# B and C products of a state space layer, taken by token quarters in four groups of 32 PSUM partitions

## The chip, the cores and the metric

The kernel is one program on one core of a Trainium2 chip. Its time is the device time in microseconds (us) of one execution; lower is better. Three runs of the kernel before gave a median of 1651.44 us, from 1648.73 to 1654.21.

## The reference, cut to what matters

A decoder layer works on x of shape (4, 1024, 256): a selective state space block, a cross attention over 154 context tokens and a mixture of eight experts, each behind a layer norm and each added to the stream. Only the first block's projections are touched:

```
xz = layernorm(x) @ W_in                 # 256 -> 1024, split into xp and z
xc = silu(causal_conv(xp))               # (4, 1024, 512)
Bm, Cm = split(xc @ W_x, 2)              # W_x is 512 x 32: 16 columns for B, 16 for C
dt = softplus(xc @ W_dt + b_dt)          # 512 x 512
h  = exp(dt * A) * h + (dt * xc) * Bm    # over 1024 tokens, 16 states for each of 512 channels
y  = sum over states of h * Cm, + D * xc
out = (y * silu(z)) @ W_out
```

## The kernel before, in words

The four batch rows are handled one after the other, in a software pipeline written out by hand. `over_rows` gives every engine the same frame: a phase for row 0, the loop of row 0, then for b = 1, 2, 3 a phase (which closes row b-1 and opens row b) and the loop of row b, then a phase that closes row 3, and the experts of row 3 alone. A phase does the matmul work outside the scan: for the closing row the gate and output products (Z, Y, O), the attention (T2, Q, PT, V), the expert input and the routing (N, G, CT); for the opening row the layer norm transposes (T), the input projection (X), the convolution, the products B, C and the step products S. The phase of row 0 has only the second part. The loop then goes over the 16 states: exponents on ScalarE, products with B on GpSimd, scans on VectorE, transposes on TensorE, sums with C on VectorE, ScalarE and GpSimd; the experts of the row before are woven in.

The order of matmul jobs in a phase is the list `all_jobs` (`alone_jobs` where no row opens); its end is `tail`. A job's PSUM bank is its place in the list modulo 8, except for those in `late_banks`. A counter `mm_ready` tells that a job is done. The reader of a job raises `act_freed` (ScalarE) or `dve_freed` (VectorE), and `wait_taken` waits for that: `wait_bank` does so for the last job in the same bank.

Around the change, in the order of `tail`:

- Job B, twice, one for each half of 512 tokens (`job_b`, L1598): `W_x` is the stationary operand, 128 rows by 32 columns for each of the four channel tiles (CT = 4), and 512 tokens of `xc` are moved past it; the sum over the four tiles stands in 32 partitions of a bank. One float32 `matmul` call becomes two weight loads and two matmul instructions in the trace, all under L1498 (`product`).
- ScalarE copies each half, 32 x 512, into `bc_sb` (L857), which is 32 partitions by 1024 tokens of `work`. Right behind these copies in ScalarE's order stand eight squares of the closing row (L863), then the exponents of the steps (L783), a table load and logarithms (L786, L789, L790), and the copies of the expert input (L800).
- Job C (`job_c`, L1609) waits for the second copy and makes eight transposes of 32 x 128 into 128 x 32 (L1615), so that tokens lie on partitions; VectorE copies the C half, 128 tokens by 8 tiles by 16 states, into `c_tok` (L1240).
- SyncE waits for the second copy, stores the 16 rows of B from `bc_sb` to `b_rows` in HBM with one DMA (L524), waits for its landing, and loads two rows of it, each broadcast to 128 partitions (`load_b`, L491), into `b_bc` and into the place of `w_out`. GpSimd waits for the first before its products `dtu` (L656).
- Eight jobs S (`job_s`, eight matmul instructions of 128 x 512 each, L1498) follow in TensorE's order. VectorE caps each (`cap`, L1113), ScalarE takes exp and ln, VectorE finishes the step (`step`, L1120). Between S jobs stand N, G and CT. In VectorE's order ahead of the first cap are the closing row's norm (L1085), the two `mean_square` (L1152), which wait for the squares, the `c_tok` copy between them, and eight instructions of the expert input (L1158), which wait for a reciprocal root on GpSimd (L619).

Of the kernel before, what the change touches and what calls it, by code (L numbers as in the profile page):

```python
# [16 lines left out]
ACT = mybir.ActivationFunctionType  # L17
# [3 lines left out]
P = 128  # L21
HALF = 512
# [6 lines left out]
def decoder_layer(nc, t, out):  # L29

    B, S, D = t["x"].shape
    DI = t["W_dt"].shape[0]
    N = t["A_log"].shape[1]
# [5 lines left out]
    DK, CT, TT = D // P, DI // P, S // P  # L39
    NH = S // HALF  # L40
# [5 lines left out]
    bd = nc.dram_tensor("b_rows", (B * N, S), F32, kind="Internal").ap()  # L46
# [9 lines left out]
    with ExitStack() as ctx:  # L56
        def sb(name, shape, dt=F32):
            return ctx.enter_context(nc.sbuf_tensor(name, shape, dt))
# [8 lines left out]
        w_x = sb("w_x", [P, CT, 2 * N])  # L67
# [14 lines left out]
        ident = sb("ident", [P, P])  # L82
# [9 lines left out]
        xc = sb("xc", [P, CT, S])  # L92
# [3 lines left out]
        c_tok = sb("c_tok", [P, TT, N])  # L96
# [4 lines left out]
        work = sb("work", [P, 10240])  # L101
# [26 lines left out]

        xp = dtu[:, :, :].rearrange("p a s -> p (a s)")[:, 0:2 * (PAD + S)].rearrange("p (r s) -> p r s", r=2)
        soft = work[:, 0:CT * NH * HALF].rearrange("p (r t) -> p r t", r=CT * NH)  # L130
        bc_sb = work[0:2 * N, 6912:6912 + S]
        TANH_AT = 8192
        NORM_AT = TANH_AT - 8 * TT
        stats = work[:, NORM_AT:NORM_AT + 6 * TT].rearrange("p (a n) -> p a n", n=6)
# [99 lines left out]
        b_stored = sem("b_stored")  # L234
# [11 lines left out]
        mm_ready = sem("mm_ready")  # L246
        act_freed = sem("act_freed")
# [50 lines left out]
        halves = range(NH)  # L298
# [4 lines left out]
        steps = [("S", d, c) for d in range(CT) for c in halves]  # L303
        LAST_STEP = CT * NH - 1

        def tiles_of(kind, c):

            if kind in ("O", "Q", "V"):
                return [(kind, c * TH + a, 0) for a in range(TH)]
            return [(kind, k, c) for k in range(CT if kind in ("Z", "Y") else DK)]  # L310

        def both(kind):
            return tiles_of(kind, 0) + tiles_of(kind, 1)

        head = [job for c in halves for kind in ("Z", "Y") for job in tiles_of(kind, c)] + both("O")
        tail = ([("B", 0, c) for c in halves] + [("C", 0, 0)] + steps[0:2] + tiles_of("N", 0) + steps[2:3] +
                tiles_of("N", 1) + steps[3:4] + [("G", 0, 0)] + steps[4:6] + [("CT", 0, c) for c in halves] + steps[6:])
        all_jobs = (head + both("T") + x_jobs((0, 1)) + both("T2") + x_jobs((2, 3)) + both("Q") + both("PT") +
                    both("V") + tail)
# [6 lines left out]
                      ("CT", 0, 0): 0, ("CT", 0, 1): 1}  # L326
        kinds_a = ("T", "X", "B", "C", "S")

        act_late = both("PT") + [("B", 0, c) for c in halves] + both("N") + [("CT", 0, c) for c in halves]
        act_order = both("T") + x_jobs((0, 1)) + both("T2") + x_jobs((2, 3)) + act_late  # L330
        act_alone = both("T2") + act_late
        dve_order = ([job for c in halves for kind in ("Z", "Y") for job in tiles_of(kind, c)] + both("O") +
# [54 lines left out]
        def wait_apart(eng, sem, value):  # L387


            eng.wait_ge(sem, value)  # L390
            eng.sem_inc(passed, 1)
# [64 lines left out]
        def _(sp):  # L456
# [38 lines left out]
            def phases(ph):  # L495
                r, b = ph.c_row, ph.a_row
                if r is not None:

                    wait_apart(sp, dbu_ready, (r + 1) * (N * CT) + DBU_CREDIT)
                    wait_apart(sp, hT_ready, (r + 1) * (N * TT) + HT_READY_CREDIT)  # L500
                    sp.dma_start(w_out[:, :, :].rearrange("p k n -> p (k n)"), w_outd).then_inc(w_out_loaded, 16)
                    load_x(r, xt, [xt_loaded, xt_loaded])
                    sp.dma_start(key_bias.rearrange("p (o f) -> p o f", o=1),
                                 k_rowd[bass.ds(r, 1), :].partition_broadcast(P)).then_inc(key_bias_loaded, 16)
                    sp.dma_start(kq[:, :, :], kqd[bass.ds(r * P, P), :].rearrange("p (k f) -> p k f", k=DK)
                                 ).then_inc(kv_loaded, 16)
                    sp.dma_start(vo[:, :, :], vod[bass.ds(r * KEYS, KEYS), :].rearrange("p (k f) -> p k f", k=2)
                                 ).then_inc(kv_loaded, 16)
                else:
                    sp.wait_ge(w_out_saved, 16)  # L510
                if r is not None and b is not None:

                    ph.wait_mm(sp, ("Y", CT - 1, NH - 1))
                    sp.sem_inc(passed, 1)
                    load_x(b, xn_a, x_in)
                if r is not None:

                    ph.wait_taken(sp, ("V", TT - 1, 0))
                    sp.dma_start(x2d[bass.ds(r * S, S), :].rearrange("(a p) d -> p a d", p=P),
                                 xt[:, :, :]).then_inc(x2_stored, 16)  # L520
                if b is not None:

                    ph.wait_taken(sp, ("B", 0, NH - 1))
                    sp.dma_start(bd[bass.ds(b * N, N), :], bc_sb[0:N, :]).then_inc(b_stored, 16)  # L524
                if r is not None:
                    wait_apart(sp, x2_stored, r * 16 + 16)
                if b is not None:
                    wait_apart(sp, b_stored, b * 16 + 16)
                    for par in range(2):
                        load_b(b, 0, 0, par)  # L530
                if r is not None:

                    ph.wait_taken(sp, ("CT", 0, NH - 1))
                    sp.dma_start(combd[bass.ds(r * E, E), :], rows[32:32 + E, :]).then_inc(comb_stored, 16)
                    wait_apart(sp, comb_stored, r * 16 + 16)
# [176 lines left out]
        def _(act):  # L712
# [52 lines left out]
            def phases(ph):  # L765
                r, b = ph.c_row, ph.a_row
# [53 lines left out]
                if r is not None:  # L820
                    for c in halves:
                        for job in tiles_of("Z", c):
                            d = job[1]
# [26 lines left out]
                if b is not None:  # L850
                    for d in (2, 3):
                        silu_tanh(d)
                    if r is None:
                        scale_weights()
                    for c in halves:
                        ph.wait_mm(act, ("B", 0, c))
                        act.activation(bc_sb[:, c * HALF:(c + 1) * HALF], ph.bank(("B", 0, c))[0:2 * N, :], ACT.Copy  # L857
                                       ).then_inc(act_freed, 1)
                if r is not None:
                    for a in range(TT):  # L860

# [36 lines left out]
                if b is None:  # L898

                    ph.wait_all_taken(act)  # L900
                else:

                    if r is not None:

                        wait_apart(act, x2_stored, b * 16)
                        wait_apart(act, x16_ready, b * TT)

                        wait_apart(act, b_stored, b * 16 + 16)

            def decay(b, alone, hf, it, par, d, opening=False, back=1):  # L910

# [134 lines left out]
        def _(dve):  # L1046
# [41 lines left out]
            def phases(ph):  # L1088
                r, b = ph.c_row, ph.a_row
# [71 lines left out]
                if r is not None:  # L1161
                    for c in halves:
# [6 lines left out]
                        for d in range(CT):  # L1169
                            job = ("Y", d, c)  # L1170
# [59 lines left out]
                if b is not None:  # L1230
                    if r is None:

                        dve.wait_ge(w_late, 7 * 16)
                        dve.tensor_scalar(w2[:, :], w2_raw, -0.5, None, ALU.mult).then_inc(dve_scaled, 1)
                        dve.tensor_copy(bias2[32:32 + E, :], bias2_raw[32:32 + E, :]).then_inc(dve_scaled, 1)
                        dve.tensor_scalar(bias1[:, :], bias1_raw[:, :], -1.0, LIMIT, ALU.mult, ALU.add
                                          ).then_inc(dve_scaled, 1)
                        dve.wait_ge(dve_scaled, 5)
                    ph.wait_mm(dve, ("C", 0, 0))
                    dve.tensor_copy(c_tok[:, :, :],  # L1240
                                    ph.bank(("C", 0, 0)).rearrange("p (a n) -> p a n", n=2 * N)[:, 0:TT, N:2 * N]
                                    ).then_inc(dve_freed, 1)
                if r is not None:
                    mean_square(1)
# [18 lines left out]
                if b is not None:  # L1263
# [13 lines left out]
                    _, d, c = steps[LAST_STEP]  # L1277
# [182 lines left out]
        def _(pe):  # L1460
# [35 lines left out]
            def product(bank, pairs):  # L1496
                for n, (left, right) in enumerate(pairs):
                    mm = pe.matmul(bank, left, right, start=(n == 0), stop=(n == len(pairs) - 1))  # L1498
                return mm
# [97 lines left out]
                mm.then_inc(mm_ready, 1)  # L1597

            def job_b(ph, r, b, job):
                c = job[2]  # L1600
                if r is None:
                    pe.wait_ge(w_early, 4 * 16)
                ph.wait_bank(pe, job)

                pe.wait_ge(xc_ready, b * CT + CT)
                product(ph.bank(job)[0:2 * N, :], [(w_x[:, d, :], xc[:, d, c * HALF:(c + 1) * HALF])
                                                   for d in range(CT)]).then_inc(mm_ready, 1)

            def job_c(ph, r, b, job):  # L1609

                ph.wait_bank(pe, job)
                ph.wait_taken(pe, ("B", 0, NH - 1))
                pe.sem_inc(passed, 1)
                for a in range(TT):
                    mm = pe.transpose(ph.bank(job)[:, a * 2 * N:(a + 1) * 2 * N], bc_sb[:, a * P:(a + 1) * P],  # L1615
                                      ident[0:2 * N, 0:2 * N])
                mm.then_inc(mm_ready, 1)

            def job_s(ph, r, b, job):
# [213 lines left out]
```

## Time and profile before

| | |
|---|---|
| median of three runs | 1651.44 us |
| the profiled execution's own time | 1651.05 us |
| span, first to last instruction | 1649.0 us |
| granted TensorE clock, mean | 0.892 |
| busy: TensorE, weight load | 1271.7 us, 839.9 us |
| busy: VectorE, ScalarE, GpSimd | 1404.2 us, 933.6 us, 969.9 us |

The span is the part of the execution between its first and its last instruction; 2.05 us lie around it. Busy times of engines overlap one another. In rows of a timeline, the first number is the start in us from the span's start, the second how long the merged group lasted, and what stands in brackets is how long the engine was idle before it and which engine, tile and line ended that. A matmul's duration includes its way through the array, so consecutive ones overlap in the records. "PE" is TensorE's matmul, "PEld" its weight load, "DVE" VectorE, "ACT" ScalarE, "POOL" GpSimd, "SP" SyncE.

### The profile page before, as it was taken

To read this page: it belongs to the slowest core of one execution; us is meant where nothing else is said; L and a number is where in the kernel's file an instruction comes from. 1 tells how busy PE (TensorE), PEld (TensorE's weight loads), DVE (VectorE), ACT (ScalarE), POOL (GpSimd) and SP (SyncE) were. 2 spreads that over 40 slices of the span, in tenths; PEclk is the share of its full clock that TensorE was granted. 3 is DMA by queue.
4 is the path that set the end of the run, shared out by engine and by line. 5 is a ranking of instruction groups with operands and counts; after the bars stand their busy time and mean duration, and the time that the engine had idled before them with its cause. 6 is when DMAs were issued, how large, how long until landed. Compare 5 with 4: busy or idle time off the path is not lost. (4 is left out here: it accounts for less than half of the span.)

```text
span 1649.0 us, 22776 instructions
## 1 busy us (share of the span) xinstructions
PE 1271.7 (77%) x5462; PEld 839.9 (51%) x5518; DVE 1404.2 (85%) x1861; ACT 933.6 (57%) x1373; POOL 969.9 (59%) x529
## 2 busy tenths in 40 slices
PE   4856667899677777899676777798877687796797
PEld 2334444564345554566354555566345454465465
DVE  6489999796899999787799999888789999973687
ACT  2454444144777777333777767523777767712554
POOL 1298888212889888321788979520588888620000
PEclk9977788999899899999899889999989989997699
DMA  7111110301111111101111111020111121010111
GB/s 226 40 39 39 39 39 26 105 1 53 59 58 38 58 52 57 62 27 54 39 59 52 44 59 63 8 87 28 65 39 58 42 67 51 25 61 26 44 59 51
DMA packets 54248, 86.47 MB, mean 52 GB/s; under 512 B 8380, under 2 KB 35141, under 8 KB 54158
## 3 DMA queue, kind: packets, MB, share of 16 engines
q1 hardware_dynamic: 50588, 83.20, 15.2%
q10 hardware_dynamic: 3570, 2.21, 0.4%
q8 instruction: 39, 0.64, 0.2%
q14 instruction: 51, 0.42, 0.1%
HBM read 74.83 MB, written 10.57 MB: 52 GB/s over the span
## 5 line engine op out<-in xcount | busy, mean ns | idle before, releaser
L1687 PE MATMUL ps<-ident,work 128*128 128x128 f32 x1536 | 307.6, 324 | 248.8 <-DVE stage L1330 169.2
L1292 DVE TENSOR_TENSOR_SCAN work<-ps,work 128x1024 f32<-128x1024 f32 x192 | 438.2, 2282 | 19.0 <-ACT ps L914 11.5
L1687 PEld LDWEIGHTS ps<-ident,work 128*128 128x128 f32 x1536 | 187.6, 159 | 385.1 <-DVE stage L1330 219.4
L914 ACT ACTIVATE ps<-dt,a_neg 128x1024 f32<-128x1024 f32 x256 | 284.7, 1116 | 116.6 <-DVE work L1292 95.1
L667 POOL TENSOR_TENSOR work<-dtu,b_bc 128x1024 f32<-128x1024 f32 x128 | 299.8, 2371 | 54.9 <-PE ps L1687 51.0
L1330 DVE SCALAR_TENSOR_TENSOR stage<-ps,c_tok,stage 128x512 f32<-128x512 f32 x384 | 271.9, 733 | 22.7 <-PE ps L1687 20.8
L1709 PE MATMUL ps<-w,work 128*128 (+1 forms) x1024 | 275.8, 419 | 2.0 <-DVE work L1437 2.0
L1709 PEld LDWEIGHTS ps<-w,work 128*128 128x128 f32 x1024 | 220.4, 217 | 54.1 <-issue 10.8
L1659 PE MATMUL ps<-nfT,w 128*128 128x512 bf16 x456 | 154.6, 429 | 40.7 <-DVE work L1367 14.8
L667 POOL TENSOR_TENSOR work<-dtu,w_out 128x1024 f32<-128x1024 f32 x64 | 149.2, 2353 | 42.1 <-PE ps L1687 42.1
L683 POOL TENSOR_TENSOR stage<-stage,work 128x512 f32<-128x512 f32 x128 | 160.1, 1275 | 14.5 <-ACT work L930 14.5
L619 POOL TENSOR_TENSOR rstd<-ve,minus_half 128x4 f32<-128x4 f32 x32 | 33.9, 1059 | 215.2 <-DVE ve L1078 198.7
L1292 DVE TENSOR_TENSOR_SCAN xt<-ps,xt 128x1024 f32<-128x1024 f32 x64 | 146.1, 2283 | 4.7 <-ACT ps L914 4.2
L667 POOL TENSOR_TENSOR xt<-dtu,w_out 128x1024 f32<-128x1024 f32 x64 | 149.8, 2362 | 0.0
L676 POOL TENSOR_TENSOR work<-work,wbc 128x1024 f32<-128x1024 f32 x48 | 112.8, 2349 | 37.0 <-DVE work L1367 37.0
L1498 PE MATMUL ps<-xnT,w_in 128*128 128x512 f32 x256 | 112.8, 594 | 2.1 <-DMA chan<-in_D_skip 1.8
L1498 PE MATMUL ps<-xc,w_dt 128*128 128x512 f32 x256 | 113.8, 597 | 0.7 <-ACT rows L887 0.7
L930 ACT ACTIVATE work<-ps,c_tok 128x512 f32<-128x512 f32 x128 | 81.9, 678 | 55.2 <-PE ps L1687 55.2
L1687 PE MATMUL ps<-ident,xt 128*128 128x128 f32 x512 | 110.0, 301 | 0.0
L1659 PEld LDWEIGHTS ps<-nfT,w 128*128 (+1 forms) x512 | 51.3, 105 | 95.3 <-issue 67.1
L656 POOL TENSOR_TENSOR dtu<-dt,xc 128x512 f32<-128x512 f32 x28 | 35.0, 1268 | 107.9 <-DVE dt L1120 107.9
L940 ACT ACTIVATE ps<-ps,bias 128x512 f32<-128x512 f32 x96 | 62.6, 652 | 40.3 <-PE ps L1659 40.3
(164 smaller groups left out, 1905.5 us busy)
## 6 DMA issues: line engine op xcount, KB each, us to landing
b_bc<-b_rows SPq DMA_DIRECT2D x32, 512.0 KB, 3.6
w_out<-b_rows SPq DMA_DIRECT2D x32, 512.0 KB, 3.9
wbc<-combine_rows SPq DMA_DIRECT2D x64, 256.0 KB, 3.3
stage<-in_x SPq DMA_DIRECT2D x8, 512.0 KB, 4.1
xt<-in_x SPq DMA_DIRECT2D x8, 512.0 KB, 6.1
x_rows<-xt SPq DMA_DIRECT2D x4, 1024.0 KB, 4.2
res<-x_rows SPq DMA_DIRECT2D x8, 512.0 KB, 3.9
out_x<-res SPq DMA_DIRECT2D x8, 512.0 KB, 3.6
```

The lines of the kernel that those rows point to most:

```text
L667: pool.tensor_tensor(slot(par, d), dtu[:, d, :], b_bcs[par], ALU.mult).then_inc(dbu_ready, 1)
L676: pool.tensor_tensor(ex_a, ex_a, wbc[:, 1 - par:2 - par, :].broadcast_to([P, 2, HALF]), ALU.mult).then_inc(aw_ready, 1)
L683: pool.tensor_tensor(stage[:, e, :], stage[:, e, :], evicted[:, e, :], ALU.add).then_inc(evict_added, 1)
L914: act.activation(decay_in(d, alone, opening), dt[:, d, :], ACT.Exp, scale=a_neg[:, bass.ds(it * 2 + (d * N + hf * (N // 2) + par), 1)]).th ...
L930: act.activation(evicted[:, e, :], ps[:, e % HT_BANKS, :], ACT.Copy, scale=c_tok[:, e, bass.ds(n, 1)]).then_inc(evict_ready, 1)
L940: act.activation(bank, bank, ACT.Relu, scale=-1.0, bias=bias1[:, bass.ds(it * 8 + (par * 4 + j), 1)]).then_inc(both_gate, 1)
L1292: dve.tensor_tensor_scan(h, decays, h, 0.0, ALU.mult, ALU.add).then_inc(scan_done, 1)
L1330: dve.scalar_tensor_tensor(stage[:, a, :], ps[:, a % HT_BANKS, :], c_tok[:, a, bass.ds(n, 1)], stage[:, a, :], ALU.mult, ALU.add).then_inc ...
L1498: mm = pe.matmul(bank, left, right, start=(n == 0), stop=(n == len(pairs) - 1))
L1659: mm = pe.matmul(ps[:, GATE_BANK + g, :], w1[:, bass.ds(wcol + k * 2 * I, P)], nfT[:, k, hf * HALF:(hf + 1) * HALF], start=(k == 0), stop= ...
L1687: mm = pe.transpose(ps[:, a % HT_BANKS, d * P:(d + 1) * P], slot(par, d)[:, a * P:(a + 1) * P], ident[:, :])
L1709: mm = pe.matmul(ps[:, 6 + a // 2, (a % 2) * D:(a % 2 + 1) * D], ex_a[:, j, a * P:(a + 1) * P], w2[:, bass.ds(col + j * D, D)], start=Fals ...
```

## The change

The four quarters of 256 tokens replace the two halves of 512. For each channel tile, four matmul calls with the same 32 weight columns move one quarter each, and quarter q goes to PSUM partitions 32q to 32q+31 of one bank. `bc_sb` becomes 128 partitions by 256 tokens and is filled by one copy. Two transposes of 128 x 128 take the place of eight of 32 x 128. The `c_tok` copy reads the same number of elements in another order. B is stored by four DMAs of 16 rows by 256 tokens, and who waited for one landing now waits for four. There is one job fewer in the list, so C moves from bank 6 to bank 5: the job S of bank 5 now waits for the `c_tok` copy, where N of bank 6 did.

```diff
-        bc_sb = work[0:2 * N, 6912:6912 + S]
+        QUARTERS = 4
+        QUARTER = S // QUARTERS
+        assert 2 * N * QUARTERS == P and QUARTER == 2 * P
+        bc_sb = work[:, 6912:6912 + QUARTER]
...
-        tail = ([("B", 0, c) for c in halves] + [("C", 0, 0)] + steps[0:2] + tiles_of("N", 0) + steps[2:3] +
+        tail = ([("B", 0, 0), ("C", 0, 0)] + steps[0:2] + tiles_of("N", 0) + steps[2:3] +
...
                 if b is not None:
-                    ph.wait_taken(sp, ("B", 0, NH - 1))
-                    sp.dma_start(bd[bass.ds(b * N, N), :], bc_sb[0:N, :]).then_inc(b_stored, 16)
+                    ph.wait_taken(sp, ("B", 0, 0))
+                    for q in range(QUARTERS):
+                        sp.dma_start(bd[bass.ds(b * N, N), q * QUARTER:(q + 1) * QUARTER],
+                                     bc_sb[q * 2 * N:q * 2 * N + N, :]).then_inc(b_stored, 16)
...
-                    wait_apart(sp, b_stored, b * 16 + 16)
+                    wait_apart(sp, b_stored, (b + 1) * (QUARTERS * 16))
...
-                    for c in halves:
-                        ph.wait_mm(act, ("B", 0, c))
-                        act.activation(bc_sb[:, c * HALF:(c + 1) * HALF], ph.bank(("B", 0, c))[0:2 * N, :], ACT.Copy
-                                       ).then_inc(act_freed, 1)
+                    ph.wait_mm(act, ("B", 0, 0))
+                    act.activation(bc_sb, ph.bank(("B", 0, 0))[:, 0:QUARTER], ACT.Copy).then_inc(act_freed, 1)
...
                     ph.wait_mm(dve, ("C", 0, 0))
-                    dve.tensor_copy(c_tok[:, :, :],
-                                    ph.bank(("C", 0, 0)).rearrange("p (a n) -> p a n", n=2 * N)[:, 0:TT, N:2 * N]
+                    dve.tensor_copy(c_tok[:, :, :].rearrange("p (q u) n -> p q u n", u=2),
+                                    ph.bank(("C", 0, 0))[:, 0:2 * P].rearrange("p (u q n) -> p q u n", u=2, q=QUARTERS
+                                                                               )[:, :, :, N:2 * N]
                                     ).then_inc(dve_freed, 1)
...
             def job_b(ph, r, b, job):
-                c = job[2]
...
-                product(ph.bank(job)[0:2 * N, :], [(w_x[:, d, :], xc[:, d, c * HALF:(c + 1) * HALF])
-                                                   for d in range(CT)]).then_inc(mm_ready, 1)
+                for d in range(CT):
+                    for q in range(QUARTERS):
+                        mm = pe.matmul(ph.bank(job)[q * 2 * N:(q + 1) * 2 * N, 0:QUARTER], w_x[:, d, :],
+                                       xc[:, d, q * QUARTER:(q + 1) * QUARTER], start=(d == 0), stop=(d == CT - 1))
+                mm.then_inc(mm_ready, 1)
...
-                ph.wait_taken(pe, ("B", 0, NH - 1))
+                ph.wait_taken(pe, ("B", 0, 0))
                 pe.sem_inc(passed, 1)
-                for a in range(TT):
-                    mm = pe.transpose(ph.bank(job)[:, a * 2 * N:(a + 1) * 2 * N], bc_sb[:, a * P:(a + 1) * P],
-                                      ident[0:2 * N, 0:2 * N])
+                for u in range(2):
+                    mm = pe.transpose(ph.bank(job)[:, u * P:(u + 1) * P], bc_sb[:, u * P:(u + 1) * P], ident[:, :])
                 mm.then_inc(mm_ready, 1)
```

## Rows read from the trace of the kernel before

**Rows 1.** Windows: us, busy (instructions) of PE, PEld, DVE, ACT, POOL; clock; DMA share; GB/s.
```profile
305.00:424.00 119.00, 109.84 (x436) 68.03 (x436) 91.25 (x228) 53.61 (x101) 32.67 (x24) 0.97 0.15 51
424.00:687.00 263.00, 193.62 (x893) 132.37 (x908) 247.02 (x230) 186.32 (x253) 219.03 (x110) 0.89 0.14 47
```

**Rows 2.** Timeline of TensorE in the phase before row 1's loop.
```profile
378.46 7.05 PE L1498 MATMUL ps<-xc,w_x 128*32 128x512 f32 x16
386.28 0.65 PE L1615 MATMUL ps<-ident,work 32*128 32x32 f32 x8 [0.77 <-ACT work L857]
386.86 7.13 PE L1498 MATMUL ps<-xc,w_dt 128*128 128x512 f32 x16
...
402.89 0.56 PE L1498 MATMUL ps<-gate_w,nfT 128*128 128x8 bf16 x16 [1.02 <-ACT nfT L800]
```

**Rows 3.** Timeline of ScalarE in the same stretch.
```profile
385.55 0.59 ACT L857 ACTIVATE work<-ps 32x512 f32<-32x512 f32 x1 [2.85 <-PE ps L1498]
386.04 0.40 ACT L863 ACTIVATE work<-xc 128x256 bf16<-128x256 bf16 x1
...
394.82 0.63 ACT L783 ACTIVATE work<-work 128x512 f32<-128x512 f32 x1 [0.81 <-DVE work L1113]
```

**Rows 4.** Timeline of VectorE in the same stretch.
```profile
383.69 1.38 DVE L1085 TENSOR_SCALAR xc<-xt,work,rstd 128x256 bf16<-128x256 f32 x4 [1.12 <-POOL rstd L619]
387.76 0.17 DVE L1152 TENSOR_SCALAR ve<-ssq 128x4 f32<-128x4 f32 x1 [2.70 <-ACT work L863]
...
389.36 0.17 DVE L1152 TENSOR_SCALAR ve<-ssq 128x4 f32<-128x4 f32 x1 [1.20 <-ACT work L863]
389.43 3.25 DVE L1158 SCALAR_TENSOR_TENSOR work<-xc,rstd,norm_w 128x256 bf16<-128x256 bf16 x8
392.60 0.74 DVE L1113 TENSOR_SCALAR work<-ps,chan 128x512 f32<-128x512 f32 x1
394.03 0.75 DVE L1113 TENSOR_SCALAR work<-ps,chan 128x512 f32<-128x512 f32 x1 [0.69 <-PE ps L1498]
...
401.91 0.75 DVE L1113 TENSOR_SCALAR work<-ps,chan 128x512 f32<-128x512 f32 x1 [2.42 <-PE ps L1498]
```

**Rows 5.** Groups of the whole trace, shapes apart: count, busy us, mean ns, idle before.
```profile
L1498 PE MATMUL ps<-w_out,xc 128*128 128x256 f32 x256 | 55.9, 379 | 0.0
L1498 PEld LDWEIGHTS ps<-w_out,xc 128*128 128x128 f32 x256 | 48.3, 190 | 6.4
L1506 PE MATMUL ps<-ident,stage 128*128 128x128 f32 x256 | 32.2, 280 | 15.4 <-DVE stage L1085 15.4
...
L1498 PEld LDWEIGHTS ps<-xc,w_x 128*32 128x32 f32 x64 | 7.0, 115 | 35.3 <-issue 35.3
...
L745 ACT ACTIVATE xc<-ps 128x256 f32<-128x256 f32 x2 | 0.8, 384 | 1.9 <-PE ps L1493 1.9
```

**Rows 6.** Timeline of GpSimd in the same stretch.
```profile
388.01 1.01 POOL L619 TENSOR_TENSOR rstd<-ve,minus_half 128x4 f32<-128x4 f32 x1 [4.36 <-DVE ve L1152]
...
398.25 2.50 POOL L656 TENSOR_TENSOR dtu<-dt,xc 128x512 f32<-128x512 f32 x2 [7.47 <-DVE dt L1120]
```

**Rows 7.** Timeline of SyncE's DMA issues in the same stretch.
```profile
386.31 0.36 SPq L524 DMA_DIRECT2D b_rows<-work  x1
388.74 0.37 SPq L491 DMA_DIRECT2D b_bc<-b_rows  x1
```

**Rows 8.** DMA issues of the page: count, KB each, median us to landing.
```profile
b_bc<-b_rows SPq DMA_DIRECT2D x32, 512.0 KB, 3.6
```

**Rows 9.** Timeline of row 0's phase: the B products, the first cap.
```profile
44.75 8.77 PE L1498 MATMUL ps<-xc,w_x 128*32 128x512 f32 x16 [14.22 <-DVE xc L1107]
...
58.56 0.75 DVE L1113 TENSOR_SCALAR work<-ps,chan 128x512 f32<-128x512 f32 x1 [3.27 <-PE ps L1498]
```

**Rows 10.** Windows of row 0's B products, columns as in group 1.
```profile
44.70:48.60 3.90, 3.85 (x5) 0.89 (x6) 2.57 (x3) 0.03 (x1) 0.00 (x0) 0.54 0.33 134
48.60:53.50 4.90, 4.90 (x12) 1.10 (x10) 0.00 (x0) 0.59 (x1) 0.00 (x0) 1.00 0.00 0
```

More of the change, by code:

```diff
@@ L327, in decoder_layer @@
         kinds_a = ("T", "X", "B", "C", "S")
-        act_late = both("PT") + [("B", 0, c) for c in halves] + both("N") + [("CT", 0, c) for c in halves]
+        act_late = both("PT") + [("B", 0, 0)] + both("N") + [("CT", 0, c) for c in halves]
         act_order = both("T") + x_jobs((0, 1)) + both("T2") + x_jobs((2, 3)) + act_late
@@ L906, in phases @@
                         wait_apart(act, x16_ready, b * TT)
-                        wait_apart(act, b_stored, b * 16 + 16)
+                        wait_apart(act, b_stored, (b + 1) * (QUARTERS * 16))
             def decay(b, alone, hf, it, par, d, opening=False, back=1):
```

## The prediction

> **What bounds the kernel now.** I read the table by stretches first, because whole-span busy shares mix two kinds of work. In a loop VectorE is busy 247 of 263 us and TensorE 194 at a lower clock; in the phase between two loops it is the other way round, TensorE 110 of 119 us at a clock of 0.97 and VectorE 91 [rows 1]. The edited jobs stand in the phases, so a microsecond saved there counts only if what follows in the phase moves with it, and the loop behind it, which cannot open before the phase's last step, then starts earlier by that much. So the second reading is the timelines of the engines from the B products to the router's products. TensorE runs almost without a gap: B from 378.46 to 385.51, 0.77 us idle for ScalarE's copy, the C transposes, then S products from 386.86 [rows 2]. Against it stand two other orders. ScalarE copies B's second half at 385.55, and eight squares sit behind that copy although their input was complete at 385.07 (383.69 + 1.38) [rows 3, 4]. VectorE waits for those squares twice (2.70 and 1.20 us), then forms the expert input, then caps S; the second cap waits 0.69 us for TensorE, the fourth 2.42 [rows 4]. So TensorE and the chain copy, squares, root, expert input, cap are nearly level here, and both begin at the end of B. In the phase of row 0 there is no closing row: the first cap waits 3.27 us for TensorE alone [rows 9].
>
> **The change, part by part.**
>
> *B products.* Removed are 16 matmul instructions of 512 columns (two halves, four channel tiles, two instructions per float32 call), added are 32 of 256 columns. Before, 7.05 us. A float32 instruction of 256 columns costs 55.9 / 256 = 0.218 us of TensorE's time, with a weight load of 0.190 us wholly beside it; its own record lasts 0.379 us, of which the rest is the way through the array [rows 5]. The trace has no case of two instructions in different column groups. So the bounds are: no overlap, 31 x 0.218 + 0.379 = 7.14 us; all four groups at once, 8 x 0.218 + 0.16 = 1.9 us; and above the first, every weight load exposed (0.115 us for 32 columns [rows 5]), 32 x (0.218 + 0.115) = 10.7 us. I take the middle kind: the groups can work side by side, but instructions start in order, and each call's second instruction must wait for its first, which uses the same group. Then the second of one quarter runs beside the first of the next, 16 turns instead of 32: 16 x 0.218 + 0.379 = 3.87 us, and B gets 3.18 us shorter. Why overlap at all: each instruction fills 32 of 128 columns, and time goes by the tokens moved, so three quarters of the array stand idle before. The nearest measured row (0.218, one after another) speaks for the other end, which is why that end keeps a good chance.
>
> The Trainium skill bears on this, for and against. Its page "TensorE: Matmul & The Clock Gate", section "Part 3: Packing small matmuls — row/col tiling", says that matmuls in different 32-column groups run concurrently while starting and ending in order, with 2.38 times the rate for three column groups; no row here shows it. By 2.38 alone B would take about 2.9 us as an estimate. Against: "TensorEngine Tiling (Array Packing)", section "Key Properties", says that a change of tiling mode drains TensorE; here the step from full-width products into the 32-column ones at 378.46 shows no idle time in the row, so I add nothing.
>
> *The copy.* Two of 32 x 512 (0.59 us each), of which the second is on the path, become one of 128 x 256: 0.384 us by a copy of the same size from PSUM [rows 3, 5]. 0.20 us saved.
>
> *C.* S starts 0.58 us after the first of eight transposes [rows 2]. Two of 128 x 128 take 2 x 32.2 / 256 = 0.25 us [rows 5]. 0.33 us saved. The `c_tok` copy has the same element count; I cost its new order at nothing, since VectorE waits for roots then anyway.
>
> *S on TensorE, middle phases.* 3.18 + 0.20 + 0.33 = 3.71 us earlier: S starts at 383.15, its second job ends at 390.28 (7.13 us [rows 2]).
>
> *The other chain.* The B copy now ends at 382.75, so the first four squares are over by 384.4, before VectorE gets to the first `mean_square`. The last four follow their inputs, 0.345 apart until 385.07; at 0.40 us each the last starts about 385.3, and `mean_square` follows it by 0.52 as before (eight squares from 386.04, the last at 388.84; then 389.36): 385.8. What is late next is the root: first `mean_square` at 385.07, root 0.25 behind it (387.76 to 388.01) and 1.01 long [rows 4, 6], expert input from 386.4, first cap 3.17 us later as before [rows 4] at 389.55, second at 389.55 + 0.70 = 390.25. Before it was 394.03: 3.78 earlier. TensorE allows 390.3 (3.7 earlier). The two agree, so a middle phase gains 3.71 if B takes 3.87 us, and never more than 3.78 however short B gets.
>
> *Later in the phase.* From the second exponent (394.82) ScalarE is full up to the expert input's copies, and those release the router's product after 1.02 us of TensorE's idleness [rows 2, 3]; this moves with the second cap. The fourth cap, bound by TensorE, moves with S. I find nothing between there and the loop that keeps its old time.
>
> *Row 0.* TensorE had been idle 14.22 us and ran the B products at a clock of 0.54, the low level of 1.2 GHz, for 3.9 us and at full clock after that; 8.77 us in all [rows 9, 10]. In 16 turns: 3.9 us hold 9.1 turns of 0.43, the other 6.9 take 1.50, the last's way 0.38, together 5.78, so 2.99 shorter, and with copy and transposes 3.52.
>
> *DMAs.* Four issues of 0.36 us instead of one put the last store 1.1 us later. The load of `b_bc` was issued 2.43 us after the store and lands after 3.6; GpSimd needs it at 398.25 [rows 6 to 8]. New: last store about 384.0, load 386.4, landed 390.0, needed at 394.5. Cost nothing; without that cover of 4.5 us it would be 1.1 us per row.
>
> *Banks.* The S job in bank 5 waits for the `c_tok` copy (385.4), long before TensorE gets there. Nothing.
>
> **Sum.** 3 x 3.71 + 3.52 = 14.65 us. The profiled execution took 1651.05 us, its span 1649.0 with 2.05 around it; it becomes 1636.4, its span 1634.35. The median of the runs is 0.39 above it, so 1636.8; I give 1636.6.
>
> **The rivals.**
>
> *All four groups at once.* B takes 1.9 us. The middle phases gain only the 3.78 of the VectorE chain; row 0 at the low clock takes 8 x 0.43 + 0.38 = 3.8 us and gains 4.97 + 0.53 = 5.5. Sum 16.8: 1634.6. Against: the pair of instructions of a call shares its group. For: S cannot show the difference, so this is close to the forecast in time. Less work in B might leave the first S products of row 0 at the low clock, which would take up to 2 us back.
>
> *No overlap: the change does not do what it says.* B 7.14 us, copy and transposes 0.53 saved: 0.44 per phase, 1.8 in all, 1649.6. For: float32 rows show one instruction after another everywhere. In the measured spread of 1648.7 to 1654.2 this could not be told from no change; about 0.3% (5 us) is what can.
>
> *Exposed weight loads, slower.* If a load into another column group waits until the running matmul is out of the array, B takes 10.7 us, S starts 3.65 - 0.53 = 3.1 us later, and as TensorE is then the later of the two chains the whole phase moves: four times 3.1, 12.4 us, 1663.8. It decides from B = 7.05 + 0.53 = 7.6 us upwards. Against: 0.190 us loads are hidden beside 0.218 us matmuls at full width. For: loads double in number, 16 to 32, and alternate between groups.
>
> **Chances.** Forecast 0.42, all four at once 0.19, no overlap 0.27, exposed loads 0.12. Faster by over 0.3% is the first two, 0.61; within 0.3% 0.27; slower 0.12. The range leaves the slow case out and little on the fast side: 1631 to 1652. The forecast's own range is 1633 to 1641.
>
> **What would show it.** In the trace after: 32 instructions in a B job with starts in pairs, the group 3.9 us from first start to end (1.9: all at once; 7.1: none; 10: exposed loads). One copy of 128 x 256 near 0.38 us. Two C transposes, S starting 0.25 us behind. Squares split in two runs of four; the first `mean_square` waiting for none; the expert input waiting for GpSimd's root; first cap 3.0 us and second cap 3.7 us nearer to the phase's start of B than before. The load of `b_bc` landing ahead of GpSimd's `dtu` with over 3 us to spare. A phase between loops of 115.3 us instead of 119. The forecast is wrong if B is over 6 us, if the second cap does not move with it, or if the loops get longer by what the phases lose.

## The result, and the profile after

The changed kernel takes 1638.03 us (median of 6 runs, 1632.91 to 1641.08) against 1651.64 us of the kernel before beside it; the ratio is 0.9913, 95% interval 0.9893 to 0.9934. In a later set the same kernel gave 1635.41 us against 1652.2 us, ratio 0.9898 (0.9877 to 0.9918). The forecast was 1636.6 us in a range of 1631 to 1652. The profiled execution took 1633.4 us with a span of 1631.4 us.

TensorE in the phase before row 1's loop, the changed kernel (start, length, engine, line, operation; in brackets the idle time before and what ended it). It answers to [rows 2]:

```profile
370.95 1.93 PE L1611 MATMUL ps<-xc,w_x 128*32 128x256 f32 x32
373.48 0.41 PE L1621 MATMUL ps<-ident,work 128*128 128x128 f32 x2 [0.60 <-ACT work L861]
373.73 7.03 PE L1502 MATMUL ps<-xc,w_dt 128*128 128x512 f32 x16
...
392.01 0.56 PE L1502 MATMUL ps<-gate_w,nfT 128*128 128x8 bf16 x16 [2.83 <-ACT nfT L805]
```

The 32 instructions of a B product take 1.93 us where 16 of twice the length took 7.05. S starts 2.78 us after B's start (8.40 before), but the router's product only 21.06 us after it (24.43 before): its wait for ScalarE grew from 1.02 to 2.83 us. S starts 5.62 us earlier and the router's product only 3.37; most of the rest (1.81 us) stands there as idle time, and 0.38 us stands ahead of N's first transposes, where TensorE waits for VectorE.

ScalarE and VectorE in the same phase, answering to [rows 3] and [rows 4]:

```profile
372.95 0.38 ACT L861 ACTIVATE work<-ps 128x256 f32<-128x256 f32 x1 [7.12 <-PE ps L1611]
373.23 0.41 ACT L866 ACTIVATE work<-xc 128x256 bf16<-128x256 bf16 x1
...
377.19 0.42 ACT L866 ACTIVATE work<-xc 128x256 bf16<-128x256 bf16 x1 [2.27 <-DVE xc L1088]
```

```profile
376.75 1.39 DVE L1088 TENSOR_SCALAR xc<-xt,work,rstd 128x256 bf16<-128x256 f32 x4 [1.12 <-POOL rstd L624]
378.04 0.17 DVE L1155 TENSOR_SCALAR ve<-ssq 128x4 f32<-128x4 f32 x1
...
378.93 0.17 DVE L1155 TENSOR_SCALAR ve<-ssq 128x4 f32<-128x4 f32 x1 [0.53 <-ACT work L866]
379.33 3.26 DVE L1161 SCALAR_TENSOR_TENSOR work<-xc,rstd,norm_w 128x256 bf16<-128x256 bf16 x8 [0.23 <-POOL rstd L624]
382.50 1.41 DVE L1116 TENSOR_SCALAR work<-ps,chan 128x512 f32<-128x512 f32 x2
```

ScalarE takes the squares in two runs of four now. The first `mean_square` waits for nothing, the expert input waits 0.23 us for GpSimd's root, and the two caps stand back to back: the second no longer waits for TensorE, whose second S product ended at 380.8. VectorE's order now holds this place alone.

SyncE and GpSimd, answering to [rows 6, 7]:

```profile
373.51 2.41 SPq L528 DMA_DIRECT2D b_rows<-work  x4
377.49 0.38 SPq L494 DMA_DIRECT2D b_bc<-b_rows  x1
```

```profile
387.38 2.49 POOL L661 TENSOR_TENSOR dtu<-dt,xc 128x512 f32<-128x512 f32 x2 [7.11 <-DVE dt L1123]
```

Now the whole stretch from B's start to the end of the last S, the three middle phases, as windows (us; busy of PE, PEld, DVE, ACT, POOL; granted clock; DMA share; GB/s). First before, then after:

```profile
378.40:418.70 40.30, 38.23 (x129) 16.07 (x128) 23.90 (x80) 25.44 (x47) 15.17 (x11) 1.00 0.25 81
760.80:801.10 40.30, 38.21 (x129) 16.07 (x128) 23.94 (x80) 25.46 (x47) 15.20 (x11) 1.00 0.24 80
1143.40:1183.70 40.30, 38.24 (x129) 16.07 (x128) 23.91 (x79) 25.43 (x47) 15.17 (x11) 1.00 0.23 80
```

```profile
370.90:407.80 36.90, 32.84 (x139) 14.85 (x138) 24.53 (x82) 24.74 (x46) 15.81 (x12) 1.00 0.27 88
749.00:786.90 37.90, 34.24 (x139) 15.54 (x138) 23.90 (x80) 24.73 (x46) 15.01 (x12) 0.95 0.26 85
1128.20:1166.10 37.90, 34.16 (x139) 15.39 (x138) 24.23 (x82) 24.79 (x46) 15.47 (x12) 0.95 0.25 85
```

The records inside give 40.20 us three times before, and 36.83, 37.87 and 37.77 after. The two longer ones have a clock of 0.95 instead of 1.00. The second shows where, in TensorE's timeline:

```profile
769.51 0.57 PE L1502 MATMUL ps<-gate_w,nfT 128*128 128x8 bf16 x16 [2.81 <-ACT nfT L805]
769.94 8.71 PE L1502 MATMUL ps<-xc,w_dt 128*128 128x512 f32 x16
```

```profile
769.75:773.16 3.41, 3.41 (x17) 1.68 (x14) 2.53 (x28) 3.36 (x5) 0.15 (x1) 0.50 0.00 0
```

The sixteen S instructions behind the idle 2.81 us take 8.71 us instead of 7.11; the granted clock (the window's third number from the end) is 0.50 for 3.41 us from 769.75 on. In row 0's phase B takes 3.64 us instead of 8.77, at half clock to its end, and from B's start to the last S 32.29 us instead of 37.80:

```profile
44.87 3.64 PE L1611 MATMUL ps<-xc,w_x 128*32 128x256 f32 x32 [14.22 <-DVE xc L1110]
49.50 13.06 PE L1502 MATMUL ps<-xc,w_dt 128*128 128x512 f32 x30
```

```profile
44.80:49.50 4.70, 4.09 (x34) 2.10 (x35) 2.59 (x3) 0.42 (x2) 0.00 (x0) 0.50 0.28 112
49.50:77.20 27.70, 27.66 (x65) 12.00 (x64) 12.19 (x14) 17.00 (x20) 9.70 (x6) 1.00 0.14 41
```

The four stretches together took 158.4 us before and take 144.8: 13.6 us less, as much as the medians of this set. A second profile of the changed kernel has 144.0, 14.4 us less, where the medians of its set differ by 16.8. All that is outside the stretches took 1490.6 us before and 1486.6 and 1489.3 in the two profiles of the changed kernel. In the ten profiles of this case, before, changed and experiments, it lies between 1486.6 and 1493.4 us, so its differences are not counted as the change's.

Row 0's stretch is less steady than the others, because the clock rises from half to full at another moment in each execution: 3.5 us after B's start in the profile before, 4.7 after the change. The run with the caps moved in the kernel before has the same phase of row 0 as that kernel; its clock rose 5.3 us after B's start, the B products took 9.65 us and the stretch 38.69. In the second profile of the changed kernel they took 3.64 and 32.06. Row 0's gain is thus 5.5 to 6.6 us by these four.

### The profile page after: what moved, and what is told of

Same layout as the page of the kernel before. It is cut to its first block and busy times, and to the rows that moved or that the text cites. A ratio compares the mean times of both kernels' runs of the same rounds, so it can differ in the third digit from the quotient of the medians.

```text
span 1631.4 us, 22872 instructions
## 1 busy us (share of the span) xinstructions
PE 1249.2 (77%) x5502; PEld 834.0 (51%) x5558; DVE 1405.1 (86%) x1861; ACT 931.2 (57%) x1369; POOL 969.0 (59%) x529
## 5 line engine op out<-in xcount | busy, mean ns | idle before, releaser
L1714 PE MATMUL ps<-w,work 128*128 (+1 forms) x1024 | 269.5, 411 | 1.8 <-DVE work L1441 1.8
L1714 PEld LDWEIGHTS ps<-w,work 128*128 128x128 f32 x1024 | 216.3, 213 | 52.6 <-issue 10.2
```

The source lines that it names most:

```text
L1714: mm = pe.matmul(ps[:, 6 + a // 2, (a % 2) * D:(a % 2 + 1) * D], ex_a[:, j, a * P:(a + 1) * P], w2[:, bass.ds(col + j * D, D)], start=Fals ...
```

## The experiments

**Order of the quarters.** Eight neighbouring instructions in one group of columns:

```diff
-                for d in range(CT):
-                    for q in range(QUARTERS):
+                for q in range(QUARTERS):
+                    for d in range(CT):
```

> The changed kernel with the 16 calls of a B product in another order: quarter by quarter, its four channel tiles in a row, so that eight neighbouring instructions use one group of 32 columns. Theory 1, overlap needs neighbours in different groups because instructions start in order: the 32 instructions follow each other every 0.218 us, the B group lasts about 7.0 us (1.93 in the changed kernel); what is left of the change is one copy and fewer transposes, 0.5 us per phase, and the time is 1649 to 1650 us. Theory 2, TensorE takes later instructions of other groups ahead: the group stays near 2 us and the time at 1638. Theory 3, most of the gain is the copy and the transposes and not the products: the group gets longer but the time stays below 1642.

1639.62 us, ratio to before 0.9923 (0.9909 to 0.9938). No theory had the size: the B product takes 4.59 us, neither 7.0 nor 2. The signs of theory 3 came (the group longer, the time below 1642), but not its cause: S starts 3.00 us earlier than in the kernel before, and 2.46 of that is B, 0.54 the copy and the transposes. TensorE, one middle phase:

```profile
373.84 4.59 PE L1611 MATMUL ps<-xc,w_x 128*32 128x256 f32 x32
379.00 0.41 PE L1621 MATMUL ps<-ident,work 128*128 128x128 f32 x2 [0.56 <-ACT work L861]
...
395.17 0.55 PE L1502 MATMUL ps<-gate_w,nfT 128*128 128x8 bf16 x16 [1.02 <-ACT nfT L805]
```

The instructions of that B product alone, in windows (us; busy and instructions touched, matmul and weight load; clock):

```profile
373.80:374.73 0.93, 0.89 (x4) 0.47 (x5) 1.00 0.00 0
374.73:375.62 0.89, 0.89 (x9) 0.53 (x8) 1.00 0.17 60
375.62:376.51 0.89, 0.89 (x10) 0.53 (x8) 1.00 1.09 387
```

In the first 0.93 us there are four instructions, one group at work; from then on about eight in 0.89 us, two groups. A quarter's eight instructions need 1.73 us one after another, yet the next quarter's start after 0.89: they run beside the last four of the first. So an instruction that finds its group busy does not hold up all that stand behind it; TensorE reaches some way ahead. That speaks against the strict order on which the forecast's 16 turns rested, and it bounds the reach, because with eight in a row it finds only one other group. (A record does not say which quarter it belongs to; the reading takes the instructions to be listed in the order of the calls.) The time says something else as well: B is 2.66 us longer than in the changed kernel, and the middle phases are 37.10 us where that had 36.83, 37.87 and 37.77:

```profile
373.80:411.00 37.20, 35.32 (x139) 16.39 (x138) 24.11 (x82) 24.67 (x46) 15.59 (x12) 1.00 0.26 87
754.10:791.30 37.20, 35.36 (x139) 16.39 (x138) 23.92 (x79) 24.62 (x46) 15.15 (x11) 1.00 0.26 86
1134.10:1171.30 37.20, 35.35 (x139) 16.39 (x138) 23.91 (x79) 24.63 (x46) 15.15 (x11) 1.00 0.24 86
```

37.10 us by the records, three times, at full clock. A phase of the changed kernel in which the clock holds takes 36.26 us (see the filled wait below), so the 2.66 us on B cost 0.8.

**Two groups at a time.**

```diff
-                for d in range(CT):
-                    for q in range(QUARTERS):
+                for d, q in [(d, p + q) for p in (0, 2) for d in range(CT) for q in range(2)]:
```

> The changed kernel with quarters 0 and 1 alternating over the four channel tiles, then quarters 2 and 3: two groups of columns at a time. Both theories of order expect the B group at 16 x 0.218 + 0.16, about 3.7 us, 1.8 us longer. Theory 1, the chain of copy, squares, root and expert input holds the second cap in the middle phases, and TensorE's wait before the router's product (2.8 us in the changed kernel) is what drops the granted clock in the phases before rows 2 and 3: S starts 1.8 us later, the wait shrinks to about 1 us, no 3.4 us at half clock in S, and each middle phase from B to the last S takes 36.4 to 36.8 us (36.8, 37.9, 37.8 in the changed kernel); only row 0's phase is about 2.4 us longer; the time is within 1 us of the changed kernel or up to 2 us faster. Rival, TensorE sets the end of these phases: all four are 1.8 to 2.4 us longer, together 8 us, 1646.

1637.04 us, ratio 0.9904 (0.9889 to 0.9919). The B product takes 2.82 us, not 3.7: again the second pair starts beside the first. Its instructions in windows, columns as above:

```profile
375.75:376.64 0.89, 0.88 (x8) 0.49 (x10) 1.00 0.00 0
376.64:377.40 0.76, 0.76 (x18) 0.53 (x16) 1.00 0.14 51
```

Eight instructions in the first 0.89 us, two groups at work, and then about sixteen in the next, four groups. In both runs the next quarters start when the busy groups come to the fifth of their eight instructions. Three instructions listed earlier are passed over then with one group busy, and six with two. So the reach is not one fixed number of instructions; a limit for each group would fit both runs, but that is inferred from two orders and not tested further.

Row 0's stretch takes 33.23 us, 0.94 more than the changed kernel's. The middle stretches take 36.27, 37.96 and 37.96 us, the last two with half clock behind a wait of 1.94 us. So the rival (TensorE sets the end) is out: S starts 0.87 us later than in the changed kernel, and 36.27 is what that takes at full clock too. Out is also the part of the theory that a wait of about 1 us would be left and the clock held: the wait was longer than I had put it because B was shorter.

**An S product in the wait.**

```diff
-                tiles_of("N", 1) + steps[3:4] + [("G", 0, 0)] + steps[4:6] +
+                tiles_of("N", 1) + steps[3:5] + [("G", 0, 0)] + steps[5:6] +
```

> The changed kernel with the fifth S product ahead of the router's product (one place in the list of jobs), into TensorE's wait of 2.8 us; the order of all other engines is kept. Theory 1 (the wait drops the clock and from the router's product to the last S TensorE sets the end): the wait goes, no half clock in these phases, the router's product starts about 1 us later, the last S ends about 2 us earlier, and a middle phase from B to the last S takes 34.5 to 36 us; the time falls by 3 to 7 us against the changed kernel. Rival, VectorE's routing (from the router's product to the fourth cap after it, 15 us) and ScalarE's logarithms set the end: the last S ends earlier but the last scan of the opening does not, the time is the same or up to 3 us slower, because routing begins 1 us later.

1639.62 us (1637.96 to 1646.29), ratio 0.9936 (0.9917 to 0.9956): no gain. The wait before the router's product is gone, and a new one stands before the transposes that need VectorE's routing:

```profile
772.13 0.55 PE L1502 MATMUL ps<-gate_w,nfT 128*128 128x8 bf16 x16
772.53 3.68 PE L1502 MATMUL ps<-xc,w_dt 128*128 128x512 f32 x8
778.22 1.40 PE L1657 MATMUL ps<-ident,work 128*8 128x128 f32 x8 [2.01 <-DVE work L1327]
780.08 8.15 PE L1502 MATMUL ps<-xc,w_dt 128*128 128x512 f32 x16 [0.46 <-ACT rows L890]
```

The half clock moved along with the wait, in two of the three phases: 8.15 us (above) and 8.83 for the last two S products instead of 7.13. The middle stretches take 36.63, 37.11 and 37.79 us; the first, at full clock, is 0.2 us below that of the changed kernel. The rival (routing holds) was the right one, but both theories had the last S ending earlier, and it hardly did.

**Eight stores of B.** Each quarter stored in two DMAs of 16 rows by 128 tokens:

```diff
                     for q in range(QUARTERS):
-                        sp.dma_start(bd[bass.ds(b * N, N), q * QUARTER:(q + 1) * QUARTER],
-                                     bc_sb[q * 2 * N:q * 2 * N + N, :]).then_inc(b_stored, 16)
+                        for h in range(2):
+                            cols = slice(q * QUARTER + h * P, q * QUARTER + (h + 1) * P)
+                            sp.dma_start(bd[bass.ds(b * N, N), cols],
+                                         bc_sb[q * 2 * N:q * 2 * N + N, h * P:(h + 1) * P]).then_inc(b_stored, 16)
```

> The changed kernel with eight stores of 16 rows by 128 tokens for B instead of four by 256. The four took 2.41 us of issue in the middle phases, not the 1.4 I had reckoned, and the load of B was issued 3.98 us behind the first. Theory 1, the stores are covered: the load is issued about 2.4 us later and lands still 3.5 us before GpSimd needs it; the time stays within 1 us of the changed kernel. Rival, B's load is near the path (row 0 above all, where its slack is smallest): up to 2 us slower in each phase, 1640 to 1646.

1635.04 us, ratio 0.9897 (0.9881 to 0.9912): no cost. SyncE in row 0's phase, where the slack is smallest, and GpSimd, which waits for the load of B before it begins:

```profile
48.81 5.00 SPq L530 DMA_DIRECT2D b_rows<-work  x8
55.02 0.36 SPq L494 DMA_DIRECT2D b_bc<-b_rows  x1
```

```profile
60.44 2.51 POOL L663 TENSOR_TENSOR dtu<-dt,xc 128x512 f32<-128x512 f32 x2 [41.91 <-DVE dt L1125]
```

GpSimd is still released by VectorE. The load took 4.1 us to landing, so it was there at 59.1, 1.3 us ahead of GpSimd (4.0 in the changed kernel) and not the 3.5 of the expectation. The four stores of the change are covered; in row 0's phase eight nearly use the cover up.

**Work in the wait that nobody needs.** Ahead of the router's product, where a row opens:

```diff
+                if b is not None:
+                    ph.wait_taken(pe, ("N", 0, 0))
+                    for k in range(2):
+                        pe.matmul(ps[:, 6, :], w_dt[:, k, 0:P], xc[:, k, 0:HALF], start=True, stop=True)
```

> The changed kernel with two extra matmul calls (four instructions of 128 x 512, 1.7 us, of results that the next product in that bank overwrites) in TensorE's wait of 2.8 us before the router's product; nothing waits for them but what stands behind them on TensorE. Theory, the wait is what drops the clock: the wait shrinks to about 1.0 us, as with quarters outermost, and no stretch of 3.4 us at half clock follows in any middle phase; from B to the last S each takes 36.2 to 36.8 us instead of up to 37.9; the time is 1 to 4 us below the changed kernel run beside it. Rival, the half clock there has another cause (it came in two or three of the middle phases of four kernels, and not always the same ones): it still comes in some, or its absence does not shorten the phase; no difference.

1634.93 us, ratio 0.9888 (0.9871 to 0.9905), beside 1635.41 for the changed kernel. In the stretch it did what the theory says, three times out of three:

```profile
373.60:409.90 36.30, 34.44 (x143) 15.55 (x142) 23.81 (x79) 24.71 (x46) 14.94 (x11) 1.00 0.26 89
752.70:789.00 36.30, 34.44 (x143) 15.55 (x142) 23.82 (x79) 24.68 (x46) 14.89 (x11) 1.00 0.27 88
1131.20:1167.50 36.30, 34.43 (x143) 15.55 (x142) 23.81 (x79) 24.71 (x46) 14.92 (x11) 1.00 0.27 89
```

36.27 us each, with four instructions more and a wait of 1.03 us. The changed kernel profiled beside it had 37.92, 37.78 and 36.26. So the wait drops the clock, in some phases and not in all, and that costs 1.5 to 1.7 us where it happens. The whole time does not show it: 0.5 us between medians whose runs spread over 4 to 8 us, and what lies outside the stretches took 1493.4 us in this profile. That the gain in the stretches is kept to the end is therefore not shown.

**The caps ahead of the second half of the expert input**, on the changed kernel and on the kernel before:

```diff
                     mean_square(1)
-                    for c in halves:
-                        expert_input(c)
+                    expert_input(0)
+                    if b is None:
+                        expert_input(1)
...
                     for i in (0, 1):
                         cap(i)
+                    if r is not None:
+                        expert_input(1)
```

> The changed kernel with VectorE's first two caps moved ahead of the second half of the expert input. Theory, after the change the middle phases are held by VectorE's order (root, expert input, caps) and no longer by TensorE: the first cap comes 1.6 us earlier, ScalarE's exponents, logarithms and copies with it, the router's product too, and TensorE's wait before it falls from 2.8 to 1.2 us; from B to the last S 34.7 to 36.3 us; the time 4 to 8 us below the changed kernel run beside it. Rival, the second half of the expert input is late for its transposes (1.4 us later, with 1.2 us of room) and the copies wait for them: half of that or nothing.

> The kernel before with the same move of the two caps. Theory, before the change the second cap waits for TensorE (0.69 us), so its time cannot come earlier: the first cap does, the second stays, ScalarE's second exponent stays, and the time is that of the kernel before within 1.5 us. Rival, VectorE's order held the phase already before the change, and the move gives the same 4 to 8 us here.

On the changed kernel: 1629.06 us (1628.09 to 1633.5), ratio to before 0.9864 (0.9844 to 0.9884), 6.3 us below the changed kernel beside it and 23 below the kernel before. By the four stretches it is 7.9 us (136.1 against 144.0). On the kernel before: 1653.43 us, ratio 1.0005 (0.9994 to 1.0016), nothing. VectorE and TensorE of the first:

```profile
381.43 1.67 DVE L1161 SCALAR_TENSOR_TENSOR work<-xc,rstd,norm_w 128x256 bf16<-128x256 bf16 x4 [0.23 <-POOL rstd L624]
383.02 1.40 DVE L1116 TENSOR_SCALAR work<-ps,chan 128x512 f32<-128x512 f32 x2
384.34 1.66 DVE L1161 SCALAR_TENSOR_TENSOR work<-xc,rstd,norm_w 128x256 bf16<-128x256 bf16 x4
```

```profile
373.61 1.93 PE L1614 MATMUL ps<-xc,w_x 128*32 128x256 f32 x32
392.53 0.56 PE L1505 MATMUL ps<-gate_w,nfT 128*128 128x8 bf16 x16 [1.24 <-ACT nfT L805]
401.17 7.13 PE L1505 MATMUL ps<-xc,w_dt 128*128 128x512 f32 x16 [0.24 <-ACT rows L890]
```

The middle stretches take 34.69, 34.69 and 34.68 us at full clock, 1.6 us below the filled wait. And in the kernel before, with the same move, the second cap waits for TensorE, now for longer than the 0.69 us of [rows 4]:

```profile
390.59 0.74 DVE L1113 TENSOR_SCALAR work<-ps,chan 128x512 f32<-128x512 f32 x1
393.60 0.75 DVE L1113 TENSOR_SCALAR work<-ps,chan 128x512 f32<-128x512 f32 x1 [2.27 <-PE ps L1501]
```

Its middle stretches stay at 40.20 us. The change and the move are worth more together than apart: short B products made VectorE's order the bound, and only then does that order matter.

**The changed kernel again**, beside the last three:

> The changed kernel as it is, beside the others on this chip, so that differences of 2 to 4 us can be read: 1633 to 1641 us, the B groups of 1.93 us, a wait of 2.8 us before the router's product in each middle phase, and 3.4 us at half clock in two or three of them.

1635.41 us; stretches of 37.92, 37.78 and 36.26 us, two with half clock. As expected.

## Why the prediction was right, and where it was not

*The forecast's number* was 14.65 us of gain; the stretches gave 13.6 and 14.4, the medians 13.6 and 16.8. The place was right: what can be told from the scatter lies between B's start and the last S, in four phases. That the number came so close is in good part luck: B was mis-sized by a factor of two, and two errors of opposite sign met in the sum.

*The B products: mis-sized.* The forecast took 3.87 us, since "each call's second instruction must wait for its first"; measured 1.93, the rival's 1.9. The step that failed is the order assumed there; the runs with other orders show TensorE going past an instruction whose group is busy. All four groups run at once when neighbours alternate over four groups (1.93 us), with two it is 2.82 us, and even eight in a row take 4.59 instead of 7.1. So of the two, the mechanism that came is that of the rival, to which I had given 0.19. The times cannot tell them apart: the rival's 1634.6 is 3.4 us from the first median and 0.8 from the later one, the forecast's 1636.6 is 1.4 and 1.2 away.

*Copy and transposes: right.* 0.384 forecast, 0.38 measured; S starts 0.25 us behind the first transpose, as forecast.

*The cap on a middle phase, "never more than 3.78 however short B gets": right in kind, 0.15 us too low.* In row 2's phase the first cap came 10.98 us after B's start (forecast 11.09), and the router's product 3.94 us earlier than before. In row 1's, VectorE was 0.6 us later against B's start than in row 2's, and only 3.37 were gained. Quarters outermost, with B at 4.59 us, gained 3.10. Where the clock held, 36.27 us was the floor with B at 1.93 and at 2.82 alike: 3.93.

*Row 0: the mechanism right, the size that of the rival.* 3.52 forecast, 5.51 measured (up to 6.6, see the result), since B took 3.64 us there where I had reckoned 5.78, and nothing else waits. The fear that S would start at half clock did not come true: the clock was full from 49.50.

*What no step had: the clock behind the wait.* Under the rival, with B at 1.9 us, I gave a middle phase no more than the 3.78 of VectorE's chain and booked TensorE's surplus as worth nothing. It was worth less than nothing: a wait of 2.8 us is followed by half clock in two of three middle phases, and costs 1.5 to 1.7 us each. The middle phases gave 3.37, 2.33 and 2.43, 8.1 us in place of 11.1. The error of 2.0 us in row 0 and this one of 3.0 nearly cancel; nothing in the prediction made them do so.

*DMAs: no cost, right; the size wrong.* In row 1's phase four issues took 2.41 us and not 1.4, and B's load was issued 3.98 us behind the first store (2.43 before). It was issued at 377.49 and took 4.2 us to landing, so it was there at 381.7, and needed at 387.4. In the other middle phases the four take less:

```profile
751.58 1.87 SPq L528 DMA_DIRECT2D b_rows<-work  x4
```

*Exposed weight loads:* none. 32 loads hide beside 1.93 us of matmuls.

*Two slips in the working.* Four squares of 0.40 us that start when the first four are over at 384.4 put the last start at 385.6, not 385.3, and the second `mean_square` at 386.1; the sum does not use it. And 7.05 / 2.38 is 2.96 us, not 2.9; the sum does not use that either.

## What to carry to other kernels

This float32 product has 32 output columns; splitting its tokens over four groups of 32 PSUM partitions, with neighbours in different groups, took it from 7.05 to 1.93 us, and made the copy behind it shorter as well. When two chains start at the same point, work out where the second one holds before shortening the first: the surplus becomes a wait, and a wait on TensorE can cost clock behind it. Then look at the order of the engine that holds now: a move that was worth nothing before the change was worth 6 us after it. All of this is one kernel on one core.

## What the hardware showed unexpectedly

- TensorE starts float32 instructions past others that are listed earlier and whose column group is busy: 4.59 us for four quarters in a row, where one after another would need about 7.1 (an estimate, 32 times 0.216 and the last record's rest). The Trainium skill, page "TensorE: Matmul & The Clock Gate", section "Part 3: Packing small matmuls — row/col tiling", says that matmuls start and end strictly in order; these times do not agree with that, unless instructions in one column group overlap, which the first four of them (one group, 0.22 us apart) do not, or the built program lists them in another order than the calls, which no record here shows.
- Four groups at once are 3.65 times as fast as the same work before (7.05 / 1.93). At half clock they take 3.64 us; no run has the old products wholly at half clock to set beside it.
- After waits of 2.8 us on TensorE 3.4 us at half clock followed in 6 of 9 middle phases (three profiles), after 1.94 to 2.01 us in 4 of 6 (two groups at a time, an S product in the wait), after 1.02 to 1.24 us in none of 15 (the kernel before with and without the caps moved, the runs with quarters outermost, with the filled wait and with the caps moved). What decides between phases with the same wait stays open.
